# Gaps of 32 to 192 bytes between SBUF tensors of a fused attention and MLP kernel

## The reference

```python
# cross attention
q = (layernorm(x) @ Wq.T).reshape(B, L, 16, 32) * 32 ** -0.5
k, v = (ctx @ Wk.T), (ctx @ Wv.T)                      # ctx: 25088 x 512
o = einsum('bhls,bshd->blhd', sigmoid(einsum('blhd,bshd->bhls', q, k)), v)
x = x + o.reshape(B, L, 512) @ Wo.T
# self attention: scores * causal mask / exp(n), no softmax; x = x + (ctx @ Wo + bo)
# MLP, ternary weights, 512 -> 2048 -> 2048 -> 2048 -> 512
h = silu(x @ w1.T * s1) * (x @ w2.T * s2)
h = gelu(h @ h1.T * sh1); h = gelu(h @ h2.T * sh2)
x = x + (h @ w3.T) * s3
```

## The kernel before

| matmuls | offset before | offset after |
|---|---|---|
| key products, L689, 4032 | 64 | 64 |
| first value product, L710, 576 | 192 | 192 |
| value products 2 to 7, L710, 3456 | 0 | 64 |
| scores, L725, 3136 | 192 | 64 |
| weighing, L742, 6272 | 0 | 0 |
| MLP layers 1 and 2, L1342 and L1357, 768 | 160 | 128 |
| MLP layer 3 with `rows`, L1357, 256 | 160 | 128 |
| MLP layer 3 with `h_lo1`, L1357, 256 | 0 | 128 |
| MLP layer 4, L1370, 64 | 96 | 128 |

## Time and profile before

### The profile page before, as it was taken

One profiled execution on the slowest core, in us unless ns is written; L12 is line 12 of the kernel. 1 busy time (PEld: TensorE's weight loads), 2 busy tenths in 40 slices (PEclk: granted clock), 3 DMA queues, 4 the chain that ended last, 5 costly groups with the idle time before them and its releaser, 6 DMA issues. The chain is left out here.

```text
span 1954.1 us, 50743 instructions
## 1 busy us (share of the span) xinstructions
PE 1939.6 (99%) x19371; PEld 1733.1 (89%) x19372; DVE 1213.4 (62%) x2113; ACT 1005.8 (51%) x1132; POOL 4.3 (0%) x16
## 2 busy tenths in 40 slices
PE   9999999999999999999999999999999999999999
PEld 7889888899888999888998888988889998857998
DVE  6576766757667676666767667576676766426322
ACT  5455454454545555454554544545455554544764
POOL 0000000000000000000000000000000000000000
PEclk9999999999999999999999999999999999999999
DMA  6656566565556656556565656655566564454774
GB/s 197 172 146 162 144 147 156 150 165 141 145 156 151 166 140 153 151 146 162 144 161 144 148 156 150 164 141 145 156 152 166 139 152 113 103 212 154 280 279 159
DMA packets 127964, 310.92 MB, mean 159 GB/s; under 512 B 33809, under 2 KB 33809, under 8 KB 108945
## 3 DMA queue, kind: packets, MB, share of 16 engines
q1 hardware_dynamic: 95808, 214.88, 43.5%
q10 hardware_dynamic: 32112, 95.43, 15.8%
HBM read 153.95 MB, written 0.52 MB: 79 GB/s over the span
## 5 line engine op out<-in xcount | busy, mean ns | idle before, releaser
L350 ACT ACTIVATE probs<-sc 128x1024 f32<-128x1024 f32 x784 | 760.9, 1024 | 745.4 <-PE sc L725 738.7
L689 PE MATMUL kp<-x_combos,weights_r 128*128 128x256 f32 x4032 | 515.1, 277 | 0.5 <-DVE k_rows_lo L532 0.5
L689 PEld LDWEIGHTS kp<-x_combos,weights_r 128*128 128x128 f32 x4032 | 484.9, 188 | 0.6 <-issue 0.6
L710 PE MATMUL vp<-more_weights,x_combos 128*128 128x256 f32 x3456 | 460.4, 283 | 0.0
L725 PE MATMUL sc<-rows_r,k_stack_r 96*128 96x256 f32 x3136 | 440.0, 283 | 1.1 <-ACT probs L350 0.8
L725 PEld LDWEIGHTS sc<-rows_r,k_stack_r 96*128 96x128 f32 x3136 | 394.5, 189 | 43.8 <-issue 41.0
L710 PEld LDWEIGHTS vp<-more_weights,x_combos 128*128 128x128 f32 x3456 | 432.6, 191 | 0.0
L742 PE MATMUL acc<-probs,v 128*32 128x256 f32 x6272 | 359.9, 381 | 0.0
L545 DVE TENSOR_TENSOR parts<-parts,kp 128x512 f32<-128x512 f32 x240 | 164.6, 686 | 284.4 <-PE kp L689 284.4
L742 PEld LDWEIGHTS acc<-probs,v 128*32 128x32 f32 x6272 | 193.4, 110 | 130.6 <-ACT probs L350 0.5
L480 DVE TENSOR_TENSOR x_combos<-ctx_raw,x_combos 128x512 fp32r<-128x512 f32 x235 | 162.6, 692 | 8.0
(11 more groups left out here) (163 smaller groups left out, 989.9 us busy)
## 6 DMA issues: line engine op xcount, KB each, us to landing
k_stack_r<-k_rows_hi SPq DMA_DIRECT2D x784, 64.0 KB, 2.4
k_stack_r<-k_rows_lo SPq DMA_DIRECT2D x784, 64.0 KB, 2.0
k_stack_r<-k_stack_r SPq DMA_DIRECT2D x196, 256.0 KB, 3.0
ctx_raw<-ctxT_dram ACTq DMA_DIRECT2D x47, 1024.0 KB, 5.8
piece<-w_all_dram ACTq DMA_DIRECT2D x176, 256.0 KB, 5.3
w_raw<-w_all_dram SPq DMA_DIRECT2D x44, 1024.0 KB, 4.7
weights<-wqk_dram SPq DMA_DIRECT2D x2, 1024.0 KB, 11.1
probs<-wkT_dram SPq DMA_DIRECT2D x1, 1024.0 KB, 5.6
```

The source lines that it names most:

```text
L350: nc.scalar.activation(probs[:, t % 2, g, :], sc[g % 2][:], ACT.Sigmoid).then_inc(probs_ready, 1)
L689: last = nc.tensor.matmul(k2[:, r, :], wk[i - 1][:, k, a, r * P:(r + 1) * P], xc[:, i - 1, k, b, :], start=i in FRESH and n == 0, stop=n = ...
L710: last = nc.tensor.matmul(v2[:, r, :], xc[:, i - 1, k, b, r * P:(r + 1) * P], wv_c[i - 1][:, k, a, :], start=i in FRESH and n == 0, stop=n ...
```

## The change

Four tensors that nothing reads or writes are put in front of others, of 64, 192, 128 and 128 bytes per partition, and one of 32 bytes. No instruction is added, removed or moved; the operands lie elsewhere.

```diff
+        def gap(name, floats):
+
+            sb(name, [P, floats])
+
+        gap("before_more_weights", 16)
         more_w = sb("more_weights", [P, 6, 2, 2, HE], F32R)
         w_of = [first_w[:, i] for i in range(8)] + [more_w[:, i] for i in range(6)]
         wk, wv_c = w_of[:7], w_of[7:]
+        gap("before_x_combos", 48)
         xc = sb("x_combos", [P, 7, 2, 2, HS], F32R)
         raw, tmp = sb("ctx_raw", [P, KE, CH]), sb("x_sum", [P, 2, HS])
 
+        gap("before_k_stack", 32)
         kst, kst_f32 = keep["two_types"](stack, "k_stack", [P, 2, 2, HG, 2, HS])
...
         h_hi = [h_hi0, keep["rows"][0][:, :, :, :].rearrange("p j g l -> p (j g) l")]
+        sb("before_h_lo1", [P, 32])
         h_lo = [h_lo0, sb("h_lo1", [P, KH, L], F32R)]
...
-                 "w_hi": sb("w_hi", [P, RING, UNIT], F32R), "w_lo": sb("w_lo", [P, RING, UNIT], F32R),
+                 "before_w_hi": sb("before_w_hi", [P, 8]), "w_hi": sb("w_hi", [P, RING, UNIT], F32R), "w_lo": sb("w_lo", [P, RING, UNIT], F32R),
```

## The result

The changed kernel takes 1943.73 us (median of 4 runs, 1943.46 to 1946.0) against 1956.2 us before: a ratio of 0.9939, with a 95% interval of 0.9921 to 0.9956. It is 12.5 us faster; forecast were 28.5.

A forecast was written before the change was run, and what follows sets the result against it. TensorE's own stream was taken to bound the kernel. Gains of 23.0 us (value products 2 to 7), 4.5 (scores) and 1.0 (MLP layer 3) sum to 28.5, taking 1955.8 to 1927 us, range 1915 to 1955.

The forecast's parts named there:

- likeliest case: Whole kernel: 28.5 us gained, to 1927 us, with its own range of 1920 to 1935; chance 0.52.
- What bounds the kernel: Time is the sum over TensorE's own stream; VectorE, ScalarE and DMAs are hidden behind it and cost nothing.
- The pair on one line: Line L769, same moving operand: 12 matmuls take 1.44 us at offset 0, 1.36 at 64; 6.7 ns per matmul at stake.
- Value products 2 to 7: 3456 matmuls going from offset 0 to 64: 1.44 to 1.36 us per product, 23.0 us gained.
- Scores: 392 groups of 8 going from offset 192 to 64: 4.5 us gained; at most 9.4 gained or 7.8 lost.
- Keys and first value product: Key products and the first value product keep their offsets: 0 us.
- MLP: All layers at new offset 128: layer 3 gains 1.0 us, layers 1, 2 and 4 taken as 0.
- Weighing: Float32 matmuls stay at offset 0, since both tensors shift by the same amount: 0 us.
- The rival of the slow phase: A phase between TensorE's read streams settles the other way, keys 1.37 to 1.41 us: 7.9 us slower, 1964 us; chance 0.13.
- a part of it: Values gain only 5.8 us, or a mixed phase with about half the groups in each gives 10; about 1946 us; chance 0.17.
- No effect: Offset merely accompanies what makes the pace, or another address bit counts; TensorE's read ports are independent: 1956 us; chance 0.08.
- The range of the likeliest case: 1920 to 1935 us: scores between nothing and 9.4 gained, MLP between 2.6 lost and 6.0 gained.

The follow-up runs named there:

- e4_sweep: Kernel before plus 2048 unused matmuls at its end: streams at sixteen operand offsets modulo 256 bytes, each entered four ways; 2196.88 us.
- e11_entries: Kernel before plus score-, key- and value-like cycles at its end: four kernels' layouts, each entered four ways and repeated six times; 2348.44 us.
- e1_values: Kernel before with only the gaps before `more_weights` and `x_combos`; 1942.52 us, ratio 0.9925.
- e2_scores: Kernel before with only the gap before `k_stack`, moving scores from offset 192 to 64; 1975.89 us, ratio 1.0095.
- e12_weigh4: e9_mlp192 with each chunk's first weighing moved from behind value product 4 to in front of it; 2127.45 us, ratio 1.0869 to the kernel before.
- e9_mlp192: Kernel before with the gaps before `more_weights` and `x_combos`, and MLP layers 1 to 3 moved to offset 192; 1935.17 us, ratio 0.9901.
- e8_order: Kernel before with the gaps of e1_values and value product 7 moved directly behind key product 7, ahead of pair 7; 1945.56 us, ratio 0.9947.

## Why the prediction was wrong

The time of 1943.7 us lies in the range of 1915 to 1955, and the sign was right, but the 28.5 us were more than twice what came, outside the likeliest case's own 1920 to 1935. By its steps:

- **What bounds the kernel**: right. Every microsecond of the difference is in TensorE's stream, and nothing waits in either kernel. That no price was due for VectorE, ScalarE and DMA holds too.
- **The pair on one line**: the reading was right as far as it went, 1.44 against 1.36 us. What I drew from it, that offset 64 has the pace of 113 ns, was the failed step: the same matmuls at it go at 113 or at 118 ns, by what ran before them (e4_sweep, e11_entries).
- **Value products 2 to 7**: forecast 23.0 us gained, measured 18.7. Products 2 to 6 gained 0.08 us each, as forecast. The seventh has the same offset and shape, and stayed slow behind scores; I said that offset and shape were enough.
- **Scores**: forecast 4.5 us gained, measured 5.9 lost, near the bound of 7.8 that I had from one early row and set aside, since "the new offset is the good one of the key products". This is the largest error, 10.4 us, and the gap before `k_stack` makes it: in the traces scores are at 115.4 to 115.7 ns behind a value product with the old offset, be that product fast (e1_values) or slow (before), and at 118.2 to 118.3 with the new one, again behind fast (changed kernel) and slow ones (e2_scores).
- **Keys and first value product**: forecast 0, measured -1.0 and +0.2.
- **MLP**: forecast 1.0 gained, measured 0.8 lost. At offset 128 all layers sit at 118.6 to 119, inside my bounds, and the sweep has 118.6 to 118.9 there from all four entries. The old offset of layers 1 and 2 has that pace too in e2_scores, so 117.3 was not theirs by offset either.
- **Weighing**: forecast 0, measured 0.4 lost.
- **The rival of the slow phase** had the right mechanism and the wrong form. I gave it one phase for the whole kernel and 0.13. It acts on each group, the changed kernel has keys at 113 ns and scores at 118 at once, and e2_scores shows what the rival forecast, 13 us in untouched keys. The likeliest case should have had the scores and product 7 at 118 ns.
- **The other rivals**: the nearest in time was a part of it, about 1946 us, in its second form, a phase that is mixed among the groups. It had 0.17, and its "about half of the groups" was a guess. No effect, with the rule on the two read ports, falls by the two value gaps, 14.7 us alone (e1_values).
- **The range of the likeliest case**: its own terms, scores at 9.4 and the MLP at 6.0 gained, give 1917.4 at the near end, not 1920. It changes nothing in the account.

## What to carry to other kernels

Where TensorE is busy throughout with float32r matmuls of 256 columns, read the distance between starts by kind and by neighbour: a spread from 113 to 120 ns between equal shapes is here a matter of where the operands lie and of what ran before. Gaps of 32 to 192 bytes add no instruction, but they can lose as well: the one before `k_stack` alone made the kernel 18.7 us slower. An edit to one pair moves the pace of others that it does not touch, so each layout is to be measured as a whole, and in several executions. A long unbroken stream is not safe either: the MLP's 1280 matmuls at offset 192 were at 113.3 ns in one program's trace and at 117.7 in another's. An order of TensorE's that is tuned to the order of VectorE's work, as here, is not free to change for a few nanoseconds a matmul: e12_weigh4 came out 192 us over e9_mlp192, for 2.5 that were to be had.

## What the runs showed of the hardware that was not expected

- Two float32r streams with the same operands, shapes and order go at 113.4 and 117.8 ns a matmul and stay so, for 24 matmuls in a row (e4_sweep), for six cycles of 32 with three changes of tensors in each (e11_entries), and for the MLP's 1280 (113.3 ns in e9_mlp192, 117.7 in e12_weigh4). Float32 matmuls of the weighing kind between them do not wipe it out (e8_order).
- No other engine is needed for the cost. From 1960 us on in e4_sweep VectorE, ScalarE and GpSimd are busy for 0.00 us and the DMA engines for 1% at most, and offset 0 is at 120 ns as in the full kernel. The Trainium skill, page "SBUF — State Buffer", section "Who interferes with whom", says that TensorE waits on no one and that its two read ports are independent; these runs show no other engine in its way, but they do show the pace of matmuls with weight loads in between changing by 6% with the distance between the two operands. Whether the SBUF side or something in the array's feeding makes it is not shown.
- The best pace found is 113.3 ns for 256 columns, with 128 or 64 stationary columns, and 227 for 512 with 128, at a granted clock of 1.00. The Trainium skill, page "TensorE: Matmul & The Clock Gate", section "Back-to-back issue gap", has a gap of N / 2.4 + 2.5 ns between isolated matmuls of N columns at full clock, which gives 109 and 216 as an estimate; no float32r stream here reached that, nor the 131 ns that the section has for a sustained stream of 512 columns.
- What rule leads from one group's phase to the next is open; the good layouts here were found by measuring places. That 256 bytes is the period fits the key products: `x_combos` lies just 256 bytes further in the changed kernel (gaps of 64 and 192), and they take 1.37 us behind scores before and 1.36 after.
